# An adaLN block with a decaying scan and a mixture of experts: the bias of the first expert layer as four products in four row tiles

## The chip, the cores and the metric

The kernel runs on one core of one Trainium2 chip. The metric is the device time of one execution in microseconds; where several runs are shown, their median counts. The core's engines work side by side and wait for one another on semaphores: PE (matrix products; its weight loads are listed as PEld), DVE and ACT (element-wise work), POOL (here element-wise work and scatters), and SP, which issues most of the DMAs.

## The reference

x has 16 batches of 512 tokens with 128 features, 8192 tokens in all. The first half of the block (layer norm, modulation, a projection, a decaying scan over the tokens, a projection back) isn't touched. In the second half each token is normalised again, and a router picks two of eight experts for it. What matters is what an expert e computes for its tokens h, with D = 128 and F = 512:

```python
p = softmax(xt @ Wr + br); probs, idx = top_k(p, 2); probs = probs / probs.sum(-1)
h = einsum('td,edf->etf', xt, W1) + b1[:, None, :]
h = layernorm(relu(h), g1, be1)
y = einsum('etf,efd->etd', h, W2) + b2[:, None, :]
y = layernorm(relu(y), g2, be2)
out = einsum('te,etd->td', gate, y)
```

The first bias b1, one row of 512 numbers per expert, is what the change is about.

## The kernel before

**Stages.** A mixer stage runs over the 16 batches (`mixer_step`, from about 0 to 165 us): it computes the first half of the block, the router, and for each token and choice a row in DRAM (`expert_rows`), sorted by expert. Then an expert stage runs over 135 tiles of 128 rows (`expert_step`, s from 0 to 141, `EXPERT_TILES` = 135); each tile belongs to one expert, whose number is known only on the chip, so engines read it into registers (`load_expert`, `load_expert_numbers`). At the end the two results of each token are weighted and added to x.

**A tile on its way.** Each engine has its own list of work for step s, written by hand; a tile passes through several steps.
- SP loads the rows of tile i (`load_rows`, line 504) into one of 8 slots, and the shifts of its expert (`load_shifts`, line 515). `load_next(i)` first waits until the tile that had the slot, i - 8, has been turned (t3_done) and has its target numbers (target_ready). Tables of row and expert numbers are read for four tiles at once.
- PE turns the rows (`turn_rows`, line 1553, for tile s + 2). ACT copies them rounded (`high_part`, h3hi, line 765), DVE makes the rest (`low_part`, h3lo, line 1140), so that the product with W1, itself in a high and a low part, keeps its precision.
- PE computes h of tile s (`hidden`, lines 1555 to 1564): b1 first, then three products of 512 columns, all into one of two PSUM banks, 1 and 2. b1's product (line 1561) multiplies a matrix of ones with `b1_parts`, a tile of 128 rows that holds b1 of all experts: row 0 its high part, row 1 its low part, zeros in the other rows.
- ACT takes h out of its bank with a relu (`hidden`, line 769, for tile s - 1, r_ready); PE turns it in four transposes (`turn_hidden`, line 1569, for tile s - 2) into bank 3 or 0; ACT copies that to rT (line 773, tile s - 3); DVE takes statistics of r (line 1145) and their mean and variance (line 1391).
- PE computes the second layer of tile s - 4 (line 1672, four products that show as eight) into bank 4 or 5; DVE scales and shifts it (`values`, line 1362, tile s - 5), ACT applies the relu (line 870), DVE takes statistics (lines 1381 and 1386), ACT takes a square root for the norms of two tiles (line 882), DVE a reciprocal, and ACT and POOL end the second norm (lines 878 and 662). POOL scatters the tile to `expert_results` (line 674).
- From tile 53 on, `piece_tile` (lines 246 to 248) spreads 44 pieces of work over the steps, each of which sums two results for 128 tokens: ACT weights the first (`early_y0g`, line 845, at the end of its step), DVE adds the second (line 1453). SP loads the results for them (line 558).

**The order on each engine.** In step s PE does h of tile s, the turn of the rows of s + 2, the second layer of s - 4, the transposes of s - 2. ACT does h3hi of s + 1, the relu of h of s - 1, the relu of s - 5, the copy to rT of s - 3, the scaling of s - 8, the square root, then a piece. DVE does the values of s - 5, the reciprocal, the scaling, h3lo, and the statistics; it ends with the targets of tile s and a piece.

**The start.** ACT fills `b1_parts` with zeros (line 747, eight copies). `split_b1` (line 749) splits b1, and SP copies the two parts into rows 0 and 1 (lines 462 and 463). Tiles 0 and 1 (`EARLY_H` = 2) are begun in the mixer's last steps: `hidden(0)` and `hidden(1)` run in its steps B and B + 1.

## Time and profile before

| | us |
|---|---|
| median of three runs | 515.25 |
| the three runs | 515.25, 514.6, 516.82 |
| the profiled execution: span from its first to its last instruction | 512.1 |
| PE busy in the span | 486.5 (95%) |
| DVE busy | 440.3 (86%) |
| ACT busy | 420.4 (82%) |
| POOL busy | 364.3 (71%) |

For the profiled execution the page gives the span; the runs' times also hold what lies before the first instruction and after the last. Busy times of PE overlap with those of its weight loads, and the products are pipelined, so the distance from one start to the next tells what a product costs, not its length. In the rows below a line is the line of the kernel before.

### The profile page before, as it was taken

What the parts mean: (1) busy time and instruction counts of PE and PEld (TensorE: products, weight loads), DVE (VectorE), ACT (ScalarE), POOL (GpSimd) and SP (SyncE); (2) the same over time, 40 slices, a digit from 0 to 9 for tenths busy, and PEclk for the clock granted to TensorE, in tenths of its full rate; (3) what the DMA queues carried; (4) which work ended last, traced back from release to release, by engine and by line L of the source; (5) the groups of instructions that cost most, each with busy time, mean ns of one, the idle gap of its engine ahead of it and who ended that gap; (6) DMA issues with size and microseconds to landing.
All of it is one profiled execution on the core that took longest, in us unless ns stands there. A gap on an engine that the chain in (4) does not pass through costs nothing. (4 is left out here: it accounts for less than half of the span.)

```text
span 512.1 us, 14684 instructions
## 1 busy us (share of the span) xinstructions
PE 486.5 (95%) x3051; PEld 386.3 (75%) x3051; DVE 440.3 (86%) x2217; ACT 420.4 (82%) x1148; POOL 364.3 (71%) x483
## 2 busy tenths in 40 slices
PE   7989999999985899999999999999999999999994
PEld 6446656555544798998989799998999989999951
DVE  7779899998887698888888799988989999898894
ACT  6678887978764688888888798899989889999883
POOL 1004665666667778888888888888888888888871
PEclk9999999999997899999999999999999999999998
DMA  6980111145111789677515785677677677567555
GB/s 166 312 240 27 44 47 48 47 131 111 55 44 52 166 154 172 188 191 198 163 64 158 187 221 152 184 205 176 164 207 191 162 189 206 151 187 214 164 173 164
DMA packets 79786, 77.78 MB, mean 152 GB/s; under 512 B 11150, under 2 KB 72745, under 8 KB 79702
## 3 DMA queue, kind: packets, MB, share of 16 engines
q1 hardware_dynamic: 71286, 59.92, 47.2%
q0 software_dynamic: 8416, 16.93, 9.2%
q8 instruction: 29, 0.48, 0.3%
q14 instruction: 55, 0.45, 0.3%
HBM read 54.65 MB, written 22.59 MB: 151 GB/s over the span
## 5 line engine op out<-in xcount | busy, mean ns | idle before, releaser
L646 POOL DMA_INDIRECT expert_rows<-rows_ring,slot x128 | 123.3, 963 | 93.6 <-issue 76.3
L674 POOL DMA_INDIRECT expert_results<-y,target x119 | 123.0, 1034 | 30.7 <-issue 26.2
L1672 PE MATMUL bank<-W,h2T 128*128 x720 | 95.4, 275 | 0.8 <-ACT h2T L773 0.3
L1672 PEld LDWEIGHTS bank<-W,h2T 128*128 128x128 f32 x720 | 87.7, 192 | 9.1 <-issue 1.4
L870 ACT ACTIVATE v<-wmod 128x128 f32<-128x128 f32 x135 | 42.0, 311 | 39.1 <-DVE vg L1373 35.5
L1362 DVE SCALAR_TENSOR_TENSOR wmod<-bank,rse,shifts 128x128 f32<-128x128 f32 x119 | 41.6, 350 | 30.8 <-PE bank L1672 25.9
L1561 PE MATMUL bank<-b_parts,onesr 128*128 x135 | 64.9, 481 | 1.2 <-DVE h3lo L1140 1.2
L758 ACT ACTIVATE n<-X,nm,rs 128x128 f32<-128x128 f32 x128 | 54.1, 486 | 8.0 <-DVE nm L1307 8.0
L1145 DVE BATCH_NORM_STATS2 stf<-h1T 128x6 f32<-128x512 f32 x90 | 59.2, 658 | 0.0
L1569 PE MATMUL bank<-ident_wr,h1T 128*128 128x128 f32 x360 | 54.5, 274 | 0.0
L1562 PE MATMUL bank<-W1hi,h3hi 128*128 x135 | 53.8, 399 | 0.0
L1563 PE MATMUL bank<-W1lo,h3hi 128*128 x135 | 53.7, 398 | 0.0
L1564 PE MATMUL bank<-W1hi,h3lo 128*128 x135 | 53.6, 397 | 0.0
L769 ACT ACTIVATE h1T<-bank 128x512 f32<-128x512 f32 x90 | 53.0, 589 | 0.2 <-PE bank L1564 0.2
L773 ACT ACTIVATE h2T<-bank 128x512 f32<-128x512 f32 x90 | 52.3, 581 | 0.1
L1672 PE MATMUL bank<-W,third_rT 128*128 x360 | 47.6, 275 | 0.8 <-ACT third_rT L773 0.8
L1672 PEld LDWEIGHTS bank<-W,third_rT 128*128 128x128 f32 x360 | 43.7, 192 | 4.9 <-issue 1.0
L1569 PEld LDWEIGHTS bank<-ident_wr,h1T 128*128 128x128 f32 x360 | 42.9, 142 | 0.3 <-issue 0.2
L1373 DVE SCALAR_TENSOR_TENSOR vg<-v,mve,shifts 128x128 f32<-128x128 f32 x119 | 42.5, 357 | 0.0
L882 ACT ACTIVATE sde<-mve,eps 128x2 f32<-128x2 f32 (+1 forms) x138 | 40.6, 295 | 0.9 <-DVE mve L1386 0.7
L1140 DVE TENSOR_TENSOR h3lo<-bank,h3hi 128x128 fp32r<-128x128 f32 x135 | 37.9, 281 | 2.8 <-ACT h3hi L765 2.8
L1381 DVE BATCH_NORM_STATS2 sty<-v 128x6 f32<-128x128 f32 x135 | 38.0, 281 | 0.3 <-ACT v L870 0.2
(250 smaller groups left out, 1229.0 us busy)
## 6 DMA issues: line engine op xcount, KB each, us to landing
shifts<-expert_shifts SPq DMA_DIRECT2D x119, 192.0 KB
hrow<-expert_rows SPq DMA_DIRECT2D x135, 65.0 KB
xi<-expert_results SPq DMA_DIRECT2D x12, 512.0 KB, 5.3
out_x<-X SPq DMA_DIRECT2D x15, 256.0 KB
X<-in_L_attn_x SPq DMA_DIRECT2D x7, 512.0 KB, 7.4
W1lo<-in_L_ffn_W SPq DMA_DIRECT2D x4, 512.0 KB, 6.7
expert_rows<-rows_ring,slot POOLq DMA_INDIRECT x128
expert_results<-y,target POOLq DMA_INDIRECT x119
```

The costliest lines, as they stand in the source:

```text
L646: nc.gpsimd.indirect_dma_start(out=rows_d, out_offset=bass.IndirectOffsetOnAxis(ap=slot[q][:, n // TOPK, n % TOPK:n % TOPK + 1], axis=0), ...
L674: nc.gpsimd.indirect_dma_start(out=results_d, out_offset=bass.IndirectOffsetOnAxis(ap=target[i % TARGETS][:], axis=0), in_=y[k], in_offset ...
L758: ins = nc.scalar.activation(dst[:, j:j + 1, :], X[:, bass.ds(b * J + j, 1), :], ACT.Identity, bias=nm_[:, x_tiles + j:x_tiles + j + 1], s ...
L769: nc.scalar.activation(r[i % DEPTH], bank[1 + i % 2][:], ACT.Relu).then_inc(r_ready, 1)
L773: nc.scalar.activation(rT[i % DEPTH], bank[3 * (1 - i % 2)][:], ACT.Copy).then_inc(rT_ready, 1)
L1145: vec.bn_stats(stf[i % 2][:], r[i % DEPTH]).then_inc(stf_ready, 1)
L1561: mm(h, onesr[:], b1_parts[:, bass.ds(e, 1), :], start=True, stop=False)
L1562: mm(h, h3hi[i % DEPTH], W1hi[:, bass.ds(e, 1), :], start=False, stop=False)
L1563: mm(h, h3hi[i % DEPTH], W1lo[:, bass.ds(e, 1), :], start=False, stop=False)
L1564: mm(h, h3lo[i % DEPTH], W1hi[:, bass.ds(e, 1), :], start=False, stop=True).then_inc(h_done, 1)
L1569: ins = tr(bank[3 * (1 - i % 2)][:, ch * P:(ch + 1) * P], r[i % DEPTH][:, ch * P:(ch + 1) * P], ident[:])
L1672: ins = mm(acc, rT[(s - 4) % DEPTH][:, ch * P:(ch + 1) * P], W2[:, bass.ds(e4 * CF + ch, 1), :], start=(ch == 0), stop=(ch == CF - 1))
```

## The change

- b1's two parts go to DRAM (`b1_two_parts`) instead of to rows of a large tile; the zeros on ACT go.
- SP loads the two rows (high and low, 4 KB) of each tile's expert into `b1_ring`, at rows 0, 32, 64 and 96 for four successive tiles, with two turns; a group of four is loaded eight tiles ahead, by `load_b1`, called in `load_next` ahead of the load of the rows. It waits for h_done of the tile eight before.
- PE issues b1's products for four tiles together (`biases`) when i is a multiple of 4: each multiplies two rows of ones with two rows of b1, each in its own quarter of the rows, each into its own bank. There are four h banks (1, 2, 3, 0) instead of two. `biases(i)` waits for the loads and for r_ready, i, which says that h of tiles up to i - 1 has been taken out.
- Turned tiles have one bank, 4, instead of two, and the second layer has one, 5; `turn_hidden` waits for the last copy to rT, and the second layer for the last values.
- In a step s that is a multiple of 4 ACT takes out h of tile s - 1 before it makes h3hi of tile s + 1.
- Some semaphores are merged (sums_stored and spare_stored go into others).

```diff
--- before.py
+++ after.py
@@ -63,6 +63,7 @@
     sums_d = nc.dram_tensor("column_sums", (2, E, D), F32, kind="Internal").ap()
     shifts_d = nc.dram_tensor("expert_shifts", (E, 3 * D), F32, kind="Internal").ap()
     gates_d = nc.dram_tensor("gate_b_rows", (1, B * D), F32, kind="Internal").ap()
+    b1_d = nc.dram_tensor("b1_two_parts", (E, 2, F), F32, kind="Internal").ap()
 
     with ExitStack() as ctx:
         def sb(name, shape, dt=F32):
@@ -116,7 +117,9 @@
         w2_sums = means[0:2, 0:E, :]
         third_rT = sb("third_rT", [P, F], F32R)
         b1hi = third_rT[0:E, :]
-        b1_parts = sb("b1_parts", [P, E, F], F32R)
+        TOGETHER = 4
+        QUARTER = P // TOGETHER
+        b1_ring = sb("b1_ring", [P, 2, F], F32R)
         onesr = sb("onesr", [P, P], F32R)
         onesf = sb("onesf", [P, P])
         WIDE = P + E
@@ -281,6 +284,27 @@
 
             return max((m for m in range(i) if ring(m) == ring(i)), default=None)
 
+        def together(i):
+
+            return range(i, min(i + TOGETHER, EXPERT_TILES))
+
+        def b1_rows(i):
+
+            first = i % TOGETHER * QUARTER
+            return slice(first, first + 2), i // TOGETHER % 2
+
+        def b1_count(i):
+
+            return 16 * sum(len(together(n)) for n in range(i % (2 * TOGETHER), i + 1, 2 * TOGETHER))
+
+        hidden_banks = [bank[n] for n in (1, 2, 3, 0)]
+
+        def hidden_bank(i):
+
+            return hidden_banks[i % len(hidden_banks)]
+
+        turned_bank, value_bank = bank[4], bank[5]
+
         early01 = [t[:].rearrange("p c l -> p (c l)").rearrange("p (j k) -> p j k", j=J) for t in xi]
         early_gb = [t[:, :].rearrange("p (j d) -> p j d", j=J) for t in scan]
         idle_rows = rows_ring[:].rearrange("p k j r -> p (k j r)")
@@ -310,10 +334,10 @@
         shifts_loaded = [sem(f"shifts_loaded{n}") for n in range(SLOTS)]
         b2_loaded = sem("b2_loaded")
         w1hi_ready, w1lo_ready = sem("w1hi_ready"), sem("w1lo_ready")
-        spare_stored = sem("spare_stored")
         pool_consts = sem("pool_consts")
         dve_setup, act_setup, pe_setup = sem("dve_setup"), sem("act_setup"), sem("pe_setup")
         gb_stored, gb_loaded, b1_stored = sem("gb_stored"), sem("gb_loaded"), sem("b1_stored")
+        b1_loaded = [sem(f"b1_loaded{n}") for n in range(2)]
 
         (n1_ready, t1_done, h1T_ready, xi0_done, xi1_done, xi0_ready, xi1_ready, z_done,
          scan_ready, mix_ready, mix_done) = [sem(n) for n in (
...
@@ -451,31 +475,31 @@
             sp.dma_start(gates_d.rearrange("o (b d) -> (o b) d", b=B), gb_raw[:]).then_inc(gb_stored, 16)
 
             sp.wait_ge(sums_copied, 2)
-            sp.dma_start(sums_d, w2_sums).then_inc(sums_stored, 16)
+            sp.dma_start(sums_d, w2_sums).then_inc(shifts_stored, 16)
             sp.dma_start(shifts_d[:, 0:D].rearrange("(o e) d -> o e d", o=1), w2_sums[0:1, :, :]).then_inc(shifts_stored, 16)
-            sp.wait_ge(sums_stored, 16)
-            sp.wait_ge(shifts_stored, 16)
+            sp.wait_ge(shifts_stored, 32)
             sp.dma_start(means[:, 0:E, :], sums_d[1:2].broadcast_to([P, E, D])).then_inc(sums_loaded, 16)
 
             sp.wait_ge(dve_setup, SETUP_END)
-            sp.wait_ge(act_setup, 3)
-            sp.dma_start(b1_parts[0:1, :, :].bitcast(F32), b1hi.bitcast(F32)).then_inc(b1_stored, 16)
-            sp.dma_start(b1_parts[1:2, :, :].bitcast(F32), b1lo[:].bitcast(F32)).then_inc(b1_stored, 16)
+            sp.wait_ge(act_setup, 2)
+            sp.dma_start(b1_d[:, 0, :], b1hi.bitcast(F32)).then_inc(b1_stored, 16)
+            sp.dma_start(b1_d[:, 1, :], b1lo[:].bitcast(F32)).then_inc(b1_stored, 16)
 
             sp.wait_ge(dve_setup, SETUP_PADDING)
             for n in range(NSPARE):
-                sp.dma_start(rows_d[SPARE + n * P:SPARE + (n + 1) * P, :], padding[:]).then_inc(spare_stored, 16)
+                sp.dma_start(rows_d[SPARE + n * P:SPARE + (n + 1) * P, :], padding[:]).then_inc(padding_stored, 16)
 
             for n, src in ((0, g2_in), (1, be2_in)):
                 sp.dma_start(second_gains[n], src).then_inc(second_gains_loaded, 16)
             sp.wait_ge(second_gains_loaded, 32)
             for n in range(2):
                 sp.dma_start(shifts_d[:, (1 + n) * D:(2 + n) * D], second_gains[n]).then_inc(shifts_stored, 16)
-            sp.wait_ge(shifts_stored, 48)
+            sp.wait_ge(shifts_stored, 64)
             sp.wait_ge(w1lo_ready, E)
 
             sp.wait_ge(table_ready, 1)
             AT_ONCE = 4
+            assert TOGETHER == AT_ONCE
             row_of, expert_of = {}, {}
 
             def load_row_numbers(i):
@@ -505,11 +529,18 @@
 
             SHIFT_LAG = SLOTS - 2
 
+            def load_b1(i):
+                load_expert_numbers(i)
+                if i == 0:
+                    sp.wait_ge(b1_stored, 32)
+                if i >= 2 * TOGETHER:
+                    sp.wait_ge(h_done, i - 2 * TOGETHER + 1)
+                for n in together(i):
+                    part, turn = b1_rows(n)
+                    sp.dma_start(b1_ring[part, turn, :].bitcast(F32), b1_d[bass.ds(expert_of[n], 1), :, :].rearrange("o k f -> (o k) f")
+                                 ).then_inc(b1_loaded[turn], 16)
+
             def load_shifts(i):
-                if i % AT_ONCE == 0:
-                    load_expert_numbers(i)
-                if i == SLOTS:
-                    sp.wait_ge(b1_stored, 32)
                 if last_user(i) is not None:
                     sp.wait_ge(y_ready, last_user(i) + 1)
                 sp.dma_start(shift_rows[ring(i)], shifts_d[bass.ds(expert_of[i], 1), :].broadcast_to([P, 3 * D])).then_inc(shifts_loaded[shift_lane(i)], 16)
@@ -517,6 +548,7 @@
             def load_next(i):
                 if i % AT_ONCE == 0:
                     load_row_numbers(i)
+                    load_b1(i)
                 sp.wait_ge(t3_done, i + 1 - SLOTS)
                 sp.wait_ge(target_ready, i + 1 - SLOTS)
                 load_rows(i, i % SLOTS)
@@ -524,6 +556,8 @@
 
             for n in range(SLOTS):
                 load_rows(n, n)
+            for n in range(0, SLOTS, TOGETHER):
+                load_b1(n)
             for n in range(SLOTS - SHIFT_LAG):
                 load_shifts(n)
             count_of = {}
@@ -574,8 +608,7 @@
             LOADED_AT = {piece_tile(b, 0) + 1: b for b in range(EARLY)}
             for i in range(ROUND1, EXPERT_TILES):
                 if i == LAST_ROWS:
-                    sp.wait_ge(spare_stored, 16 * NSPARE)
-                    sp.wait_ge(padding_stored, 16 * E)
+                    sp.wait_ge(padding_stored, 16 * (NSPARE + E))
                     rows_of_batches(B)
                 load_next(i)
                 if i in GB_AT:
@@ -742,10 +775,7 @@
 
             act.wait_ge(c_loaded, 16)
             nc.scalar.activation(c_act[:], c_sb[:], ACT.Silu).then_inc(act_setup, 1)
-            act.wait_ge(dve_setup, SETUP_PADDING)
-            for e in range(E):
-                ins = nc.scalar.activation(b1_parts[:, e, :], padding[:, TAGS:TAGS + 1].broadcast_to([P, F]), ACT.Copy)
-            ins.then_inc(act_setup, 1)
+
             def split_b1():
                 act.wait_ge(gains_loaded, 80)
                 act.wait_ge(dve_setup, SETUP_PADDING)
@@ -766,11 +796,11 @@
 
             def hidden(i):
                 act.wait_ge(h_done, i + 1)
-                nc.scalar.activation(r[i % DEPTH], bank[1 + i % 2][:], ACT.Relu).then_inc(r_ready, 1)
+                nc.scalar.activation(r[i % DEPTH], hidden_bank(i)[:], ACT.Relu).then_inc(r_ready, 1)
 
             def hidden_turned(i):
                 act.wait_ge(tr_done, i + 1)
-                nc.scalar.activation(rT[i % DEPTH], bank[3 * (1 - i % 2)][:], ACT.Copy).then_inc(rT_ready, 1)
+                nc.scalar.activation(rT[i % DEPTH], turned_bank[:], ACT.Copy).then_inc(rT_ready, 1)
 
             def mixer_step(s, q, e, k):
                 if on(s, B):
@@ -855,11 +885,14 @@
 
             def expert_step(s, n):
                 q = n % 2
+                last_of_group = s % TOGETHER == 0
+                if last_of_group and on(s - 1, EXPERT_TILES) and s - 1 >= EARLY_H:
+                    hidden(s - 1)
                 if on(s + 1, EXPERT_TILES) and s + 1 >= EARLY_H:
                     high_part(s + 1, bank[7 - q][:, 0:P])
                 if s == 1:
                     half_gates()
-                if on(s - 1, EXPERT_TILES) and s - 1 >= EARLY_H:
+                if not last_of_group and on(s - 1, EXPERT_TILES) and s - 1 >= EARLY_H:
                     hidden(s - 1)
                 if on(s - 3, EXPERT_TILES) and s >= EXPERT_TILES:
                     hidden_turned(s - 3)
@@ -972,7 +1005,7 @@
                 vec.tensor_scalar(be1_g1m[:, :, 1], bank[7][:, 0:E * CF], 1.0 / F, None, ALU.mult)
                 mark(vec.tensor_copy(be1_g1m[:, :, 0], bank[7][:, E * CF:2 * E * CF]))
                 assert done[0] == SETUP_SUMS
-                dve.wait_ge(act_setup, 3)
+                dve.wait_ge(act_setup, 2)
                 mark(vec.tensor_tensor(b1lo[:], b1f[:], b1hi, ALU.subtract))
                 assert done[0] == SETUP_END
 
@@ -1359,7 +1392,7 @@
                 dve.wait_ge(y_done, s - 4)
                 dve.wait_ge(shifts_loaded[shift_lane(s - 5)], 16 * shift_uses(s - 5))
                 dve.wait_ge(rse_ready, s - 4)
-                vec.scalar_tensor_tensor(wide(v0[p]), wide(bank[4 + p][:, 0:D]), rse[q][:, 0:1],
+                vec.scalar_tensor_tensor(wide(v0[p]), wide(value_bank[:, 0:D]), rse[q][:, 0:1],
                                          wide(shift_rows[k5][:, 0:D]), ALU.mult, ALU.add).then_inc(v0_ready, 1)
 
             def reciprocals(s, p):
@@ -1552,21 +1585,30 @@
                 pe.wait_ge(hrow_loaded[row_slot], (i + SLOTS - row_slot) * (16 // SLOTS))
                 tr(to, hrow[row_slot][:, H], ident[:]).then_inc(t3_done, 1)
 
+            def biases(i):
+                pe.wait_ge(b1_loaded[i // TOGETHER % 2], b1_count(i))
+                pe.wait_ge(r_ready, i)
+                for n in together(i):
+                    part, turn = b1_rows(n)
+                    mm(hidden_bank(n)[:], onesr[part, :], b1_ring[part, turn, :], start=True, stop=False)
+
             def hidden(i):
-                e, q = expert_of[i], i % 2
-                h = bank[1 + q][:].rearrange("p (o f) -> p o f", o=1)
+                e = expert_of[i]
+                h = hidden_bank(i)[:].rearrange("p (o f) -> p o f", o=1)
+                if i == 0:
+                    pe.wait_ge(h3lo_ready, EARLY_H)
+                if i % TOGETHER == 0:
+                    biases(i)
                 pe.wait_ge(h3lo_ready, i + 1)
-                if i >= 2:
-                    pe.wait_ge(r_ready, i - 1)
-                mm(h, onesr[:], b1_parts[:, bass.ds(e, 1), :], start=True, stop=False)
                 mm(h, h3hi[i % DEPTH], W1hi[:, bass.ds(e, 1), :], start=False, stop=False)
                 mm(h, h3hi[i % DEPTH], W1lo[:, bass.ds(e, 1), :], start=False, stop=False)
                 mm(h, h3lo[i % DEPTH], W1hi[:, bass.ds(e, 1), :], start=False, stop=True).then_inc(h_done, 1)
 
             def turn_hidden(i):
                 pe.wait_ge(r_ready, i + 1)
+                pe.wait_ge(rT_ready, i)
                 for ch in range(CF):
-                    ins = tr(bank[3 * (1 - i % 2)][:, ch * P:(ch + 1) * P], r[i % DEPTH][:, ch * P:(ch + 1) * P], ident[:])
+                    ins = tr(turned_bank[:, ch * P:(ch + 1) * P], r[i % DEPTH][:, ch * P:(ch + 1) * P], ident[:])
                 ins.then_inc(tr_done, 1)
 
             def mixer_step(s, q, e, k):
@@ -1661,10 +1703,10 @@
                     load_expert(s + 1)
                 if on(s - 4, EXPERT_TILES):
                     e4 = expert_of[s - 4]
-                    acc = bank[4 + q][:, 0:D].rearrange("p (o d) -> p o d", o=1)
+                    acc = value_bank[:, 0:D].rearrange("p (o d) -> p o d", o=1)
                     pe.wait_ge(rT_ready, s - 3)
-                    if on(s - 6, EXPERT_TILES):
-                        pe.wait_ge(v0_ready, s - 5)
+                    if on(s - 5, EXPERT_TILES):
+                        pe.wait_ge(v0_ready, s - 4)
                     if s == TABLE2_STEPS:
                         pe.wait_ge(spread_ready, 2)
                         mm(bank[5][:, TABLE:TABLE + 2 * P], onesf[:], spread[:].rearrange("p t i -> p (t i)"), start=True, stop=True).then_inc(spread_done, 1)
```

## Rows read from the trace of the kernel before

**Rows 1.** Section 1 of the page: busy us of each engine, share of the span, instructions.
```profile
PE 486.5 (95%) x3051; PEld 386.3 (75%) x3051; DVE 440.3 (86%) x2217; ACT 420.4 (82%) x1148; POOL 364.3 (71%) x483
```

**Rows 2.** Windows, expert stage: busy us (x instructions) PE, PEld, DVE, ACT, POOL; clock, DMA.
```profile
172.00:488.00 316.00, 315.15 (x2256) 284.85 (x2254) 279.00 (x1245) 277.36 (x829) 265.06 (x373) 1.00 0.68 177
```

**Rows 3.** Timeline of PE, one step: start us, us, engine, line, op [idle before <-releaser].
```profile
299.97 0.60 PE L1569 MATMUL bank<-ident_wr,h1T 128*128 128x128 f32 x4
...
302.34 0.60 PE L1569 MATMUL bank<-ident_wr,h1T 128*128 128x128 f32 x4
302.69 0.47 PE L1561 MATMUL bank<-b_parts,onesr 128*128 x1
303.00 0.39 PE L1562 MATMUL bank<-W1hi,h3hi 128*128 x1
...
303.70 0.27 PE L1553 MATMUL bank<-ident_wr,hrow 128*128 128x128 f32 x1
303.81 1.06 PE L1672 MATMUL bank<-W,h2T 128*128 x8
304.70 0.60 PE L1569 MATMUL bank<-ident_wr,decay 128*128 128x128 f32 x4
```

**Rows 4.** Timeline of PE and its loads: transposes of 32 rows; full loads.
```profile
17.31 0.60 PE L1539 MATMUL bank<-ident_wr,n 128*128 128x128 f32 x4
...
17.84 0.13 PEld L1522 LDWEIGHTS bank<-ident_wr,rows_ring 32*128 32x128 f32 x1 [0.17 <-issue]
...
17.90 0.14 PEld L1523 LDWEIGHTS bank<-ident_wr,rows_ring 32*128 32x128 f32 x1
...
302.67 0.19 PEld L1561 LDWEIGHTS bank<-b_parts,onesr 128*128 128x128 f32 x1
...
302.78 0.19 PEld L1562 LDWEIGHTS bank<-W1hi,h3hi 128*128 128x128 f32 x1
```

**Rows 5.** Timeline of DVE and ACT in the steps of rows 3.
```profile
300.17 0.35 DVE L1362 SCALAR_TENSOR_TENSOR wmod<-bank,rse,shifts 128x128 f32<-128x128 f32 x1 [0.35 <-PE bank L1672]
...
301.82 0.16 DVE L1386 BATCH_NORM_AGGREGATE mve<-sty 128x2 f32<-128x6 f32 x1
...
302.22 0.26 ACT L765 ACTIVATE h3hi<-bank 128x128 fp32r<-128x128 f32 x1
...
302.38 0.59 ACT L769 ACTIVATE h1T<-bank 128x512 f32<-128x512 f32 x1
...
302.54 0.35 DVE L1362 SCALAR_TENSOR_TENSOR wmod<-bank,rse,shifts 128x128 f32<-128x128 f32 x1
...
303.52 0.58 ACT L773 ACTIVATE h2T<-bank 128x512 f32<-128x512 f32 x1
...
304.59 0.39 ACT L845 ACTIVATE n<-xi,gate 128x128 f32<-128x128 f32 x1
...
304.88 0.26 ACT L765 ACTIVATE h3hi<-bank 128x128 fp32r<-128x128 f32 x1
```

**Rows 6.** Timeline of ACT and PE at the last tiles.
```profile
487.43 0.57 ACT L773 ACTIVATE h2T<-bank 128x512 f32<-128x512 f32 x1
...
488.15 1.22 PE L1672 MATMUL bank<-W,h2T 128*128 x8 [0.28 <-ACT h2T L773]
```

**Rows 7.** SP's waits in total (us, times, longest); timelines: an SP issue, a late row load.
```profile
SPq L515 <- POOL y L662: 96.4, 85, 9.9
...
305.65 0.33 SPq L504 DMA_DIRECT2D hrow<-expert_rows  x1
...
291.29 0.33 PE L1553 MATMUL bank<-ident_wr,hrow 128*128 128x128 f32 x1 [0.25 <-DMA hrow<-expert_rows]
```

**Rows 8.** Timeline of ACT and DVE at the start.
```profile
3.43 4.26 ACT L747 ACTIVATE b_parts<-padding 128x512 fp32r<-128x512 f32 x8 [0.81 <-DVE padding L940]
...
7.15 0.16 DVE L1307 SCALAR_TENSOR_TENSOR nm<-mv,rs 128x4 f32<-128x4 f32 x1
```

**Rows 9.** Timeline of PE's weight loads, end of the mixer stage.
```profile
159.57 0.42 PEld L1539 LDWEIGHTS bank<-ident_wr,n 128*128 128x128 f32 x4 [0.55 <-ACT n L758]
```

More of the change, by code:

```diff
@@ L334, in adaln_ssm_moe_kernel @@
         rows_stored = [sem(f"row_group_stored{m}") for m in range(ROW_LANES)]
-        sums_done, sums_copied, sums_stored, sums_loaded, w2_ready = (
-            sem("sums_done"), sem("sums_copied"), sem("sums_stored"), sem("sums_loaded"), sem("w2_ready"))
+        sums_done, sums_copied, sums_loaded, w2_ready = (
+            sem("sums_done"), sem("sums_copied"), sem("sums_loaded"), sem("w2_ready"))
         count_done, counts_ready, table_step, spread_ready, spread_done, table_ready, padding_stored = (
```

## The prediction

> **What bounds the kernel now.** I read the busy shares first: PE is at 95%, DVE, ACT and POOL lie under it [rows 1]. A share is a mean over stages, so I asked for the stretch in which the expert tiles run: from 172 to 488 us PE is busy 315.15 of 316.00 us at a granted clock of 1.00, while DVE and ACT are busy 279 and 277 [rows 2]. In that stretch PE is the bound and the others wait for it. The timeline of PE then gives the step of one tile [rows 3]: transposes of r at 302.34, b1's product at 302.69, three W1 products from 303.00, the turn of the next rows at 303.70, the second layer at 303.81, the next tile's transposes at 304.70. That is 2.36 us from transposes to transposes, with no idle time noted on any row; 133 tiles at 2.36 make 314 us, which is the stretch.
>
> **The change, part by part. b1's product leaves the step.** The start noted for the first product of a tile comes early, since its weights are still being loaded; so I take the pitch of the three behind it: 303.70 - 303.00 = 0.70, 0.233 each [rows 3]. Tiles 2 to 134 lose one each: 133 x 0.233 = **-31.0 us**. Nothing on PE covers it, so all of it lies on the path; the step becomes 2.13.
>
> **Four b1 products together, 33 times** (before tiles 4, 8, ..., 132). No product in four row tiles stands in the trace, so I bound it. From below: one load and one product's pitch, all four side by side, no cost for going over to row tiles and back: 0.06 + 0.23 = 0.29. From above: one load at the full pitch, four products one after the other, and a drain: 0.11 + 4 x 0.23 + 0.09 = 1.12. The nearest rows are the two transposes of 32 rows, which also use only part of the array's rows [rows 4]. They show two things. The load for the second starts 0.06 after the load for the first (17.84, 17.90), while full loads stand 0.11 apart (302.67, 302.78). And the first 32-row load starts only at 17.84, though four transposes at 0.11 each from 17.31 have fed their last column by 17.75: 0.09 for draining before the change of rows, and the trace notes no engine that it waited for. I take loads one after the other at 0.06, products side by side, and one drain on the way back: 4 x 0.06 + 0.23 + 0.09 = **0.56 per group**. The drain on the way in is hidden by the wait that comes next; without that cover 0.09 more.
>
> A rule of the Trainium skill, page "TensorE: Matmul & The Clock Gate", section "LDWEIGHTS (loading the stationary operand)", says that a load's time goes with its columns and that 32 rows take as long as 128. By that rule the four loads cost 0.44 instead of 0.24 and the sum is that of the rival of slow loads, below. The 0.06 in the trace speaks against it, but it is one pair of loads.
>
> **A new wait on PE.** The four products write all four h banks, so they wait (r_ready, i) until ACT has taken out the h of the tile just before. PE's transposes at 299.97 stand two steps before the b1 product at 302.69 [rows 3]; without b1's product in between, PE is there after 2.72 - 0.23 = 2.49 us. ACT's chain in the same time [rows 5]: DVE's values start at 300.17, released by PE's second layer; DVE's last statistics of the step start at 301.82; ACT's step ends with a square root of them, and its next step starts at 302.22, 2.25 after the transposes. There h3hi comes first now and h at 302.38; the change puts h first in each fourth step, so h is out at 2.25 + 0.59 = 2.84. From ACT's end to PE's next load the tail of the trace shows 488.15 - (487.43 + 0.57) = 0.15 [rows 6], with a register operation in between, which the four products do not have; with 0.10, PE starts at 2.94. **The wait is 2.94 - 2.49 = 0.45 per group** (0.40 to 0.50). The chain hangs on PE's own second layer two steps back, for which DVE was waiting (0.35 idle), so a faster PE does not shorten it. Behind the wait stands all of PE's work and, through it, DVE's and ACT's; SP and POOL run ahead. Where ACT also does y0g in the step before (304.59, with the next start at 304.88), the wait grows by 0.29; by lines 246 to 248 this is so for seven groups (after tiles 83, 87, ..., 107): +2.0 us. In the fourth step h3hi goes up to 0.59 later; its reader on PE is a step away.
>
> **The other waits.** One bank for turned tiles: PE's transposes also wait for the last rT. ACT's copy ends at 303.52 + 0.58 = 304.10, the transposes start at 304.70 [rows 3, 5]; ACT's copy follows DVE's values, and these PE's step, so that of 0.60 at least 0.37 stays. One bank for values: DVE is done at 302.54 + 0.35, PE wants the bank at 303.81: 0.92 of cover. If a cover fell short by 0.1 in every step it would cost 13 us; I see no reason for it. At the end, where PE's steps have no hidden layer, the single bank bites: the last transposes must wait for ACT's copy until 488.00, and the second layer of 488.15 goes back by their length [rows 6]: +0.3 us (0 to 0.5).
>
> **SP and the DMAs.** 135 loads of 4 KB come in, four per group, at SP's place just before the load of tile i's rows; reading the experts' numbers moves there too, and h_done of tile i-8 is awaited there. Behind it stand the rows of tile i and the shifts of tile i-6. SP waits 96.4 us for POOL's y alone, and 135 issues of 0.33 are 45 us [rows 7]; target_ready of tile i-8, awaited there already, comes later than h_done. I cost it at nothing. If the cover fails, rows come late as at 291.29, 0.25 idle [rows 7]: at the eleven early loads of results (line 558) up to 11 x 0.25 = 2.8 us.
>
> **Start and change of stage.** ACT's eight fills of b1_parts (4.26 us from 3.43, so until 7.69) go; ACT's next work waits for nm, ready at 7.15 + 0.16 [rows 8]: -0.2 us (0 to -0.4). The first group is issued in the mixer's last steps and waits for the second h3lo; soon after, PE idles 0.55 at 159.57 for ACT [rows 9], which covers that and the products. Without that cover, up to 0.5.
>
> **The sum.** -31.0 + 33 x (0.56 + 0.45) + 2.0 + 0.3 - 0.2 = +4.4 us. It is made against the profiled execution, a span of 512.1; the timed runs stand at 514.6 to 516.82, about 3 us above it, and I add the difference to their median: 515.25 + 4.4 = **519.7 us**. With the bounds of the wait and of the late ends this case holds 516.5 to 524. A measurement here tells about 0.5%, 2.6 us, from no change. So the group's price decides: at 0.43 nothing changes, under 0.35 it is faster by 0.5%, over 0.50 slower by it.
>
> **Rivals.**
> *Loads side by side too.* Different rows of the array could load at once: 0.11 + 0.23 + 0.09 = 0.43, 33 x -0.13 = -4.3, 515.4 us, no change. For it: the 0.06 was for two loads into the same rows, so it need not hold between different rows. Against it: no full loads overlap in the trace. The same page of the Trainium skill, section "Measured speedup vs the span model", gives four row tiles 3.07 times the speed of one after the other; by it, as an estimate, 4 x 0.23 / 3.07 + 0.09 = 0.39 and 514.1 us. No row here shows four.
> *Faster.* Everything side by side and no drain: the lower bound, 0.29, 33 x -0.27 = -8.9, 510.8 us. The wait remains even so, which is why there is no more to be had. For it: the 0.09 may belong to something else than the change to 32 rows. Against it: it is the place where PE goes to fewer rows at full clock, and it shows the gap.
> *Slow loads.* Four at 0.11: 0.76, 33 x 0.20 = +6.6, 526.3 us. For it: every full load that follows another stands 0.11 behind it. Against it: the pair at 0.06.
> *The change doesn't do what it says.* The products run one after the other: 1.12, 33 x 0.56 = +18.5, 538.2 us. For it: the products of 512 columns in these rows are 0.23 or more apart. Against it: those use the whole array.
>
> **Chances.** Forecast 0.40, loads side by side 0.22, faster 0.12, slow loads 0.12, one after the other 0.14. The wait's uncertainty (0.05 x 33 = 1.7 us) spreads the first two over the bounds of 0.5%: faster by over 0.5% 0.12 + 0.06 = 0.18, within 0.24, slower by over 0.5% 0.58. The range goes from 510.0, just past the faster case, to 530.0, past slow loads; it leaves out products one after the other and a little at each end, under 0.2.
>
> **What would show it.** Right: no b1 product in three of four steps, and those steps at 2.13; in the fourth, PE idle 0.35 to 0.5 ahead of its load, released by ACT's relu (longer where y0g stands before it), four products whose starts are some 0.06 apart, and the first W1 load 0.56 after the first b1 load; DVE's wait for PE shorter in three steps. Wrong: no idle time there (the chain through DVE was not tight), starts 0.23 apart (no row tiles), steps without b1 longer than 2.13 (DVE, ACT or a bank took over), or rows that come late.

## The result and the profile after

The changed kernel takes 520.69 us (median of four runs, 519.55 to 522.04) against 515.42 (514.6 to 516.82) for the kernel before beside it: a ratio of 1.0103, 95% interval 1.0074 to 1.0131. It is slower by about 1%, 5.3 us; the forecast was 4.4 us slower. The profiled execution ran 521.47 us with a span of 519.6. That is 7.5 us above the span of 512.1 before: the two profiled executions lie further apart than the medians, and what is read from the profiles below adds up to these 7.5.

In the new lines, b1's products are L1593, the W1 products L1603 to L1605, the turn of the rows L1586, the second layer L1714, the transposes of r L1611; on ACT h3hi is L795, the relu of h L799, y0g L875.

The busy times of the page, and the same window as in [rows 1, 2]:

```profile
PE 483.3 (93%) x3051; PEld 371.7 (72%) x3051; DVE 442.1 (85%) x2217; ACT 413.8 (80%) x1140; POOL 360.9 (69%) x483
172.00:488.00 316.00, 302.40 (x2200) 261.72 (x2199) 273.70 (x1216) 268.89 (x813) 255.39 (x364) 1.00 0.67 176
```

In the expert stage PE, idle for 0.85 us before, now stands idle for 316.00 - 302.40 = 13.6 us, and fewer instructions fit into the same window, on every engine. The timeline of PE, a step without b1 and a step with a group, answers [rows 3]:

```profile
346.04 0.60 PE L1611 MATMUL bank<-ident_wr,h1T 128*128 128x128 f32 x4
346.39 0.48 PE L1603 MATMUL bank<-W1hi,h3hi 128*128 x1
...
347.18 0.27 PE L1586 MATMUL bank<-ident_wr,hrow 128*128 128x128 f32 x1
347.29 1.05 PE L1714 MATMUL bank<-W,third_rT 128*128 x8
348.18 0.60 PE L1611 MATMUL bank<-ident_wr,h1T 128*128 128x128 f32 x4
349.04 0.51 PE L1593 MATMUL bank<-b_ring,onesr 2*128 2x512 f32 x4 [0.27 <-ACT h1T L799]
349.48 0.49 PE L1603 MATMUL bank<-W1hi,h3hi 128*128 x1
...
351.29 0.60 PE L1611 MATMUL bank<-ident_wr,decay 128*128 128x128 f32 x4
```

The step without b1 takes 348.18 - 346.04 = 2.14, as worked out. The step with a group takes 351.29 - 348.18 = 3.11, 0.97 more. All four products together last 0.51 from the first start to the last end, hardly longer than one alone (0.47 in [rows 3]): they run side by side. PE's weight loads at the same place:

```profile
349.01 0.22 PEld L1593 LDWEIGHTS bank<-b_ring,onesr 2*128 2x128 f32 x4 [0.47 <-issue]
349.48 0.19 PEld L1603 LDWEIGHTS bank<-W1hi,h3hi 128*128 128x128 f32 x1 [0.25 <-issue]
```

The four loads also run side by side: 0.22 for all four, against 0.19 for one full load. From the first of them to the next full load it is 0.47, of which 0.25 is idle time of the loads without a releaser. The products run in this time, 0.23 for one by its pitch, so the 0.25 is not the price of the way back alone. From the first b1 product to W1 it is 0.44, 0.21 more than one product's pitch; how much of that is loads and how much the way back isn't told apart. ACT's timeline shows what PE waits for, at this group and at one with y0g before it:

```profile
348.12 0.29 ACT L915 ACTIVATE sde<-mve,eps 128x2 f32<-128x2 f32 x1
348.31 0.59 ACT L799 ACTIVATE h1T<-bank 128x512 f32<-128x512 f32 x1
348.78 0.28 ACT L795 ACTIVATE h3hi<-bank 128x128 fp32r<-128x128 f32 x1
...
387.80 0.39 ACT L875 ACTIVATE n<-xi,gate 128x128 f32<-128x128 f32 x1
388.09 0.57 ACT L799 ACTIVATE h1T<-bank 128x512 f32<-128x512 f32 x1
```

The square root, then h, first in the step, out at 348.90; PE's load follows at 349.01. Where y0g stands between them, PE's row is

```profile
388.81 0.50 PE L1593 MATMUL bank<-b_ring,onesr 2*128 2x512 f32 x4 [0.56 <-ACT h1T L799]
```

an idle time of 0.56 instead of 0.27. Two rows of a tile come late, as in [rows 7] but by more:

```profile
293.25 0.33 PE L1586 MATMUL bank<-ident_wr,hrow 128*128 128x128 f32 x1 [0.59 <-DMA hrow<-expert_rows]
...
299.09 0.33 PE L1586 MATMUL bank<-ident_wr,hrow 128*128 128x128 f32 x1 [0.80 <-DMA hrow<-expert_rows]
```

**Where the time went.** I add up the distances between starts on PE from tile 4's first W1 product to tile 134's, 130 steps:

| | us |
|---|---|
| before | 310.1 |
| b1's product gone from 130 steps, 0.227 each | -29.5 |
| 32 groups: last transpose to first b1 product, and from there to W1, 33.8 in all, less the 0.03 that a step without a group has there | +32.9 |
| before and after the turn of the rows (late rows) | +2.0 |
| small delays elsewhere (what is left over) | +1.5 |
| after | 317.0 |

The median distance from one tile's first W1 product to the next tile's tells the kernels apart (g: the step into a tile whose b1 products come first in a group; each profile has some longer steps besides):

| kernel | step | step g | g in every |
|---|---|---|---|
| before | 2.37 | | |
| after | 2.15 | 3.15 | 4th |
| groups of four, the last h taken out early | 2.16 | 2.76 | 4th |
| groups of three, no wait | 2.16 | 2.75 | 3rd |
| groups of two, no wait | 2.16 | 2.75 | 2nd |

### The profile page after: what moved, and what is told of

The parts are those of the page before. It is cut to its first block and busy times, and to the rows that moved or that the text cites. A ratio compares the mean times of both kernels' runs of the same rounds, so it can differ in the third digit from the quotient of the medians.

```text
span 519.6 us, 14981 instructions
## 1 busy us (share of the span) xinstructions
PE 483.3 (93%) x3051; PEld 371.7 (72%) x3051; DVE 442.1 (85%) x2217; ACT 413.8 (80%) x1140; POOL 360.9 (69%) x483
## 5 line engine op out<-in xcount | busy, mean ns | idle before, releaser
L707 POOL DMA_INDIRECT expert_results<-y,target x119 | 120.2, 1010 | 30.0 <-issue 24.0
L1714 PE MATMUL bank<-W,h2T 128*128 x720 | 95.5, 276 | 1.1 <-issue 0.6
L1714 PEld LDWEIGHTS bank<-W,h2T 128*128 128x128 f32 x720 | 87.5, 191 | 10.0 <-issue 2.3
L1603 PE MATMUL bank<-W1hi,h3hi 128*128 x135 | 66.6, 494 | 0.7 <-DVE h3lo L1173 0.7
L1611 PE MATMUL bank<-ident_wr,h1T 128*128 128x128 f32 x360 | 54.4, 274 | 0.0
L1605 PE MATMUL bank<-W1hi,h3lo 128*128 x135 | 54.1, 401 | 0.0
L799 ACT ACTIVATE h1T<-bank 128x512 f32<-128x512 f32 x90 | 52.8, 587 | 1.1 <-PE bank L1605 1.1
L1714 PE MATMUL bank<-W,third_rT 128*128 x360 | 47.8, 276 | 1.0 <-DVE wmod L1395 0.8
L1714 PEld LDWEIGHTS bank<-W,third_rT 128*128 128x128 f32 x360 | 43.7, 191 | 5.7 <-issue 1.8
L1611 PEld LDWEIGHTS bank<-ident_wr,h1T 128*128 128x128 f32 x360 | 42.1, 142 | 0.9 <-issue 0.4
L1586 PE MATMUL bank<-ident_wr,hrow 128*128 128x128 f32 x135 | 36.9, 276 | 1.4 <-DMA hrow<-expert_rows 1.4
```

Source lines behind the costliest of these rows:

```text
L707: nc.gpsimd.indirect_dma_start(out=results_d, out_offset=bass.IndirectOffsetOnAxis(ap=target[i % TARGETS][:], axis=0), in_=y[k], in_offset ...
L799: nc.scalar.activation(r[i % DEPTH], hidden_bank(i)[:], ACT.Relu).then_inc(r_ready, 1)
L1603: mm(h, h3hi[i % DEPTH], W1hi[:, bass.ds(e, 1), :], start=False, stop=False)
L1605: mm(h, h3lo[i % DEPTH], W1hi[:, bass.ds(e, 1), :], start=False, stop=True).then_inc(h_done, 1)
L1611: ins = tr(turned_bank[:, ch * P:(ch + 1) * P], r[i % DEPTH][:, ch * P:(ch + 1) * P], ident[:])
L1714: ins = mm(acc, rT[(s - 4) % DEPTH][:, ch * P:(ch + 1) * P], W2[:, bass.ds(e4 * CF + ch, 1), :], start=(ch == 0), stop=(ch == CF - 1))
```

## The experiments

**1. Four products in one row tile.** Are the row tiles worth what they seem?

```diff
 def b1_rows(i):
-    first = i % TOGETHER * QUARTER
-    return slice(first, first + 2), i // TOGETHER % 2
+    return slice(0, 2), i % (2 * TOGETHER)
```

> The changed kernel with one edit: b1's two rows of all four tiles lie at row 0, so the four products of a group use the same row tile. Theory 1 (row tiles make the products run side by side): in the changed kernel the group takes 0.44 us from the first b1 load to the first W1 load, starts 0.003 apart; here starts 0.21 to 0.23 apart, the group 0.11 + 4 x 0.23 + 0.09 = 1.12, so 33 x 0.68 = +22 us over the changed kernel's 520.7: about 543 us. Rival (the group's price is the going over to few rows and back, whichever rows they are): starts and price as in the changed kernel, 520.7 us.

548.66 us (546.97 to 550.1), ratio 1.0651 (1.0612 to 1.0691). Timeline of PE (lines are one lower here):

```profile
301.53 1.16 PE L1592 MATMUL bank<-b_ring,onesr 2*128 2x512 f32 x4 [0.31 <-ACT h1T L798]
302.62 0.50 PE L1602 MATMUL bank<-W1hi,h3hi 128*128 x1
```

In one row tile the four last 1.16 together and W1 follows 302.62 - 301.53 = 1.09 after the first; in four row tiles it is 0.44. 33 times 0.65 is 21.5 of the 28.0 us; in the expert stage the granted clock is also 0.98 in this profile, not 1.00, which is about 6 us of 316. Theory 1 holds, with 28 us instead of 22: the row tiles do what they say.

**2. The relu of h in its old place.**

```diff
-    last_of_group = s % TOGETHER == 0
+    last_of_group = False
```

> The changed kernel without its last part: ACT makes h3hi first and takes out h after it in every step. Theory 1 (PE waits at each group for h of the tile before, at the end of the chain second layer, DVE, ACT): h comes out one h3hi later, 0.16 us by the starts of the two, so PE's wait grows from 0.48 to 0.64 per group: 33 x 0.16 = +5.3 us, about 526 us. Rival (PE's wait ends on something else, the b1 loads or PE's own queue): no change, 520.7 us within 1.5.

528.41 us (526.89 to 530.98), ratio 1.0275 (1.023 to 1.0321). The waits of this kernel, and those of the changed kernel (us, times, longest):

```profile
PE bank L1593 <- ACT h1T L799: 11.1, 21, 0.9
PE bank L1593 <- ACT decay L799: 5.8, 11, 0.9
```

```profile
PE bank L1593 <- ACT h1T L799: 7.7, 21, 0.7
PE bank L1593 <- ACT decay L799: 3.7, 11, 0.6
```

The new order on ACT is worth 7.7 us, 5.5 of them (16.9 - 11.4) in this one wait. PE does hang on ACT's relu, and the length of ACT's work ahead of it sets the wait.

**3. The wait without the products, and neither.** Both leave b1 out of h.

```diff
 for n in together(i):
     part, turn = b1_rows(n)
-    mm(hidden_bank(n)[:], onesr[part, :], b1_ring[part, turn, :], ...)
+    pass
 ...
-mm(h, h3hi[i % DEPTH], W1hi[...], start=False, stop=False)
+mm(h, h3hi[i % DEPTH], W1hi[...], start=True, stop=False)
```

> The changed kernel without the four b1 products (b1 is left out of the result); the waits ahead of them stay. Theory 1: the group's 0.44 goes, the wait of 0.48 stays: 520.7 - 33 x 0.44 = about 506 us. Rival (the products hide in the wait or the wait grows in their place): 515 us or more.

514.02 us (512.63 to 515.64), ratio 0.9976 (0.996 to 0.9992): 6.7 us less than the changed kernel, half of the 14 expected, and between the two cases. Timeline of PE, two late rows and a group:

```profile
271.20 0.33 PE L1586 MATMUL bank<-ident_wr,hrow 128*128 128x128 f32 x1 [1.85 <-DMA hrow<-expert_rows]
...
275.70 0.47 PE L1586 MATMUL bank<-ident_wr,hrow 128*128 128x128 f32 x1 [0.53 <-DMA hrow<-expert_rows]
...
310.24 0.60 PE L1611 MATMUL bank<-ident_wr,h1T 128*128 128x128 f32 x4
311.14 0.49 PE L1603 MATMUL bank<-W1hi,h3hi 128*128 x1 [0.29 <-issue]
```

At the group, 0.90 from the transposes to W1 instead of 0.35 elsewhere (346.39 - 346.04): the wait alone is 0.55. Over the 25 groups from tile 8 on that have no y0g ahead of them the median is 0.54; in the changed kernel, with the products, the same 25 have 0.48. So the wait is there without the products, and they don't lengthen it. The steps with a group fall from 3.15 to 2.75 in the median, as the price of the products says; but with faster steps two rows come later, and those two steps take 5.13 and 4.07, 4.9 us more than 2.15 each.

The second kernel loosens the wait as well, to `pe.wait_ge(r_ready, i - 3)`, which one bank needs.

> The changed kernel without the four b1 products (b1 is left out of the result) and with the wait loosened to what a bank needs: h of four tiles before instead of one. Theory 1: the wait's 0.48 per group goes too, and the longer waits at pieces on ACT with it, 33 x 0.48 + 4 = 20 us less than with the wait: about 486 us, 133 steps of 2.14. Rival (without the wait DVE or ACT bounds the step, so that the wait costs little by itself): within 6 us of the kernel that keeps the wait, 500 us or more.

505.62 us (504.5 to 507.7), ratio 0.9818 (0.9777 to 0.9859): the wait is worth 8.4 us here, not the 20 of theory 1, and a little more than the rival's 6. Timeline of PE, then windows (PE, PEld, DVE, ACT, POOL; clock, DMA):

```profile
263.78 0.39 PE L1606 MATMUL bank<-W1hi,h3lo 128*128 x1
270.90 0.48 PE L1586 MATMUL bank<-ident_wr,hrow 128*128 128x128 f32 x1 [6.74 <-DMA hrow<-expert_rows]
271.47 2.07 PE L1715 MATMUL bank<-W,third_rT 128*128 x8
...
200.00:266.00 66.00, 64.11 (x473) 57.78 (x472) 59.29 (x262) 59.10 (x177) 55.48 (x72) 1.00 0.66 169
266.00:276.00 10.00, 5.01 (x18) 3.92 (x18) 3.94 (x18) 3.48 (x11) 8.60 (x12) 0.52 0.39 111
```

One row comes 6.74 late, and after this idle time PE's granted clock is at its lower level, 1.2 GHz: the second layer takes 2.07 instead of 1.05. So even a kernel with no b1 at all gains only 9.4 us over the one before, where 133 products of 0.227 are 30. PE's steps are not all that stands behind the time. SP's and POOL's timelines show what made this row late:

```profile
250.56 0.33 SPq L528 DMA_DIRECT2D hrow<-expert_rows  x1
267.40 0.33 SPq L546 DMA_DIRECT2D shifts<-expert_shifts  x1
267.96 0.33 SPq L528 DMA_DIRECT2D hrow<-expert_rows  x1
...
252.96 0.47 POOL L695 TENSOR_TENSOR xi<-wmod,mixT_both 128x128 f32<-128x128 f32 x1
257.55 0.46 POOL L695 TENSOR_TENSOR xi<-win,scan 128x128 f32<-128x128 f32 x1
```

SP's load of shifts waits for POOL's y of an earlier tile, and the loads of rows stand behind it. POOL works through its own list, two tiles in 257.55 - 252.96 = 4.59 us, so 2.3 a tile, with no idle time over 0.3 between its instructions there: nearly the 2.37 of PE's step in the kernel before, and more than the 2.15 here. In every kernel here but that of experiment 1, whose PE is the slowest, POOL's store of tile 42's results begins at 291.0 to 292.4 us, and at tile 56 none is ahead of the kernel before: the first W1 product of that tile starts at 298.3 there and at 299.7 in this one. The 9.4 us all come behind it. That POOL's list holds PE back up to there is read from the traces; no run took work from POOL.

**4. h of a group's last tile taken out early.** ACT does that relu in the step before, behind the copy to rT and ahead of the scaling and the square root. Products and group stay.

```diff
+    if (s + 1) % TOGETHER == 0 and s + 1 < EXPERT_TILES:
+        hidden(s)
```

> The changed kernel with one edit on ACT: h of the last tile of a group is taken out one step earlier in ACT's list, after the copy to rT and ahead of the scaling and the square root, so ahead of ACT's wait for DVE. Theory 1 (the wait of 0.48 per group hangs on the chain second layer, DVE's statistics, ACT's square root, h): h is out before PE arrives, PE's wait falls to 0.1 or less, 33 x 0.4 + 4 = -14 to -19 us: 502 to 507 us; DVE's reciprocal comes up to 0.3 later in one step of four, which DVE's wait for PE covers. Rival (the square root now comes 0.48 late and DVE hands it on to PE's second layer): the wait moves to the second layer and half or more of it stays, 512 to 521 us.

515.66 us (514.85 to 516.78, 12 runs), ratio 1.0006 (0.9995 to 1.0018): 5.0 us less than the changed kernel, in the rival's range and not in that of theory 1. The wait is gone, at every group. Timeline of PE and two windows of this kernel, then one of the changed kernel (PE, PEld, DVE, ACT, POOL; clock, DMA):

```profile
450.08 0.63 PE L1611 MATMUL bank<-ident_wr,h1T 128*128 128x128 f32 x4
450.64 0.51 PE L1593 MATMUL bank<-b_ring,onesr 2*128 2x512 f32 x4
451.08 0.50 PE L1603 MATMUL bank<-W1hi,h3hi 128*128 x1
...
172.00:180.00 8.00, 8.00 (x30) 6.34 (x30) 3.90 (x20) 3.28 (x9) 6.15 (x7) 0.50 0.72 169
360.00:480.00 120.00, 119.77 (x867) 102.87 (x866) 114.60 (x486) 107.39 (x333) 97.97 (x155) 1.00 0.70 195
```

```profile
172.00:180.00 8.00, 7.77 (x59) 6.77 (x58) 5.60 (x29) 5.63 (x16) 6.02 (x7) 1.00 0.81 175
```

With no releaser named, PE still starts the first b1 product 0.20 after the last transpose (median of 32 groups), where W1 starts 0.03 after it in other steps. That is 0.17 for going over to row tiles, which the wait had covered before. A group then costs 0.17 + 0.44 = 0.61 beyond the plain step, and four tiles save 0.91: 33 x 0.61 - 133 x 0.227 = -10 us should remain against the time of before. They don't. Three things in this profile stand against it. PE runs at the lower clock from 172 to 180 us, right behind the change of stage with its short stretches of work between waits: 30 products there against 59 in the changed kernel (last row). From tile 66 on the step before a group takes 2.35 to 2.41 instead of 2.14 in 10 of 17 cases, and some steps with a group are longer by 0.1: DVE is busy 114.60 of 120 us there, and the second layer and the transposes, which have one bank each, start a little late. And one row comes late (1.4 us in its step). By the steps' lengths these are some 3.4, 3.7 and 1.4 us; that the single banks are what passes DVE's and ACT's lateness on was not tried by itself. Nor does the clock decide it. The mean granted clock is 0.972 to 0.975 in five of the twelve runs and 0.978 to 0.981 in seven, and both take 515.8 us in the mean. The last kernel of experiment 7 has the same early relu and a clock of 0.99 from 172 to 180 us; its steps from tile 46 to 54, where rows come late, are 6 us longer in all, and it takes the same time. What fits both is POOL's pace up to tile 56: there this kernel starts at 299.0, against 298.3 before, and from there to tile 134 it takes 184.7 us, against 184.8.

**5. Three together on four banks.** A group of three leaves a bank over, so that its products need only the tile before the last (`pe.wait_ge(r_ready, i - 1)`); ACT keeps the order of before. b1's rows are loaded by threes too, two tiles later in SP's list.

```diff
-    TOGETHER = 4
+    TOGETHER = 3
...
-    pe.wait_ge(r_ready, i)
+    pe.wait_ge(r_ready, i - 1)
```

> The changed kernel with groups of three tiles on the four h banks: the products of a group then need h of the tile two before, not of the tile just before. ACT takes out h in its old place. Theory 1 (a group's wait is what eats the gain): no wait, 0.43 for each of 44 groups, so against the kernel before -31 + 44 x 0.43 = -12 us: about 503 us. Rival (each going over to row tiles costs PE more than the trace shows, or DVE and ACT bound the step): 512 us or more.

514.48 us (513.46 to 516.33, 12 runs), ratio 0.999 (0.9977 to 1.0003): the wait is gone here too, and no more is gained. Timeline of PE and a window:

```profile
335.61 0.60 PE L1612 MATMUL bank<-ident_wr,h1T 128*128 128x128 f32 x4
336.14 0.50 PE L1594 MATMUL bank<-b_ring,onesr 2*128 2x512 f32 x3
336.57 0.50 PE L1604 MATMUL bank<-W1hi,h3hi 128*128 x1
...
172.00:180.00 8.00, 8.00 (x43) 6.67 (x43) 4.59 (x23) 4.41 (x14) 6.17 (x7) 0.73 0.87 164
```

Three products cost the same 0.43 as four, so 44 groups at 0.60 give 26.4 back of the 30.2 saved. Theory 1 left the way in out of its price, and the 3.8 us that are left should show; 0.8 do, with an interval that holds no change. The clock stands at 0.73 behind the change of stage, but here too the time doesn't follow the mean clock of the run (four at 0.975 and 0.976 take 513.5 to 514.2, seven at 0.978 and 0.979 take 514.2 to 515.7, one at 0.972 takes 516.3).

**6. Two together.** If a group has a price of its own, groups of two must lose. Like experiment 5, with 67 groups, each in two row tiles (`pe.wait_ge(r_ready, i - 2)`, `for n in range(i, min(i + 2, EXPERT_TILES))`); b1's rows are loaded by fours, two tiles later than in the changed kernel.

> b1's products in groups of two, 67 of them, on four banks, with no wait for the tile just before, and ACT in the order of before. Theory (a group costs PE some 0.61 us beyond a step without it, whatever it holds: 0.17 for draining on the way in and 0.43 for products and the way back): 22 or 23 groups more than in groups of three, 14 us more than those 514.5, so 526 to 530 us; transposes to first b1 product 0.20 and first b1 product to first W1 product about 0.42. Rival (the price goes with the products in the group): groups of two cost half, 512 to 517 us.

526.65 us (526.05 to 526.9), ratio 1.0219 (1.0198 to 1.024). Timelines of PE and of its loads:

```profile
301.03 0.60 PE L1613 MATMUL bank<-ident_wr,decay 128*128 128x128 f32 x4
301.56 0.50 PE L1595 MATMUL bank<-b_ring,onesr 2*128 2x512 f32 x2
301.99 0.50 PE L1605 MATMUL bank<-W1hi,h3hi 128*128 x1
...
303.79 0.60 PE L1613 MATMUL bank<-ident_wr,h1T 128*128 128x128 f32 x4
...
305.94 0.27 PE L1613 MATMUL bank<-ident_wr,h1T 128*128 128x128 f32 x1
...
301.56 0.18 PEld L1595 LDWEIGHTS bank<-b_ring,onesr 2*128 2x128 f32 x2 [0.17 <-issue]
301.99 0.19 PEld L1605 LDWEIGHTS bank<-W1hi,h3hi 128*128 128x128 f32 x1 [0.25 <-issue]
```

The same 0.43 and the same 0.17 and 0.25 of idle loads, for two products. A step with a group is 2.76 long, one without 2.15: 0.61, 67 times, is 40.9, less 30.2 saved: 10.7 us slower, and 11.2 were measured. The price hangs on the group, not on what is in it; the rival (half the price for half the products) is out.

**7. Three smaller suspects.** The piece of y0g behind h and not ahead of it, in the steps with a group:

> The changed kernel with one edit on ACT: where a piece of the results' sum stands at the end of the step before a group, it is done after h is taken out instead. Theory 1 (such a piece lengthens PE's wait by 0.29 to 0.35 at the seven groups after tiles 83 to 107, where the wait reads 0.8 to 0.98 instead of 0.48): -2 to -3 us, 517.7 to 518.7. Rival (the longer waits there come from something else, such as DVE's sums): 520.7 within 1.

519.74 us (517.31 to 522.47), ratio 1.0082 (1.0053 to 1.011), against 1.0103 (1.0074 to 1.0131) for the changed kernel. By its time this is the rival's case, though the intervals overlap. The traces settle the wait itself: at the seven groups the way from the last transpose to the first b1 product falls from 0.82 to 1.00 in the changed kernel to 0.48 to 0.71 here, 1.8 us in all. So y0g does lengthen the wait there, by 0.25 in the mean; in the time it doesn't show.

b1's loads issued on SP behind the tile's rows and shifts, and not ahead of them:

> The changed kernel with one edit on SP: the four b1 loads of a group are issued behind the row and shift loads of tile i instead of ahead of them. Theory 1 (SP's four more issues stand ahead of the rows after a big load of results and make two row loads later, PE's wait for rows grows from 0.5 before to 1.9 in the changed kernel): about 1 us less, 519 to 520. Rival (the rows come late from the big loads of results alone): no change, and PE's wait for rows stays at 1.4 or more.

521.22 us (519.66 to 523.62), ratio 1.0126 (1.01 to 1.0153): no gain, though no wait of PE names the load of rows in this profile (one turn of rows has 0.58 of idle time ahead of it without a releaser). These late loads together with the early relu of experiment 4, as the version that might beat both kernels:

> The version with h of a group's last tile taken out early, and b1's rows loaded after the tile's rows and shifts. Theory (late rows are one of the delays that ate the gain of the early relu): no wait of PE for hrow, 513 to 515 us, just below the time of before. Rival (what ate it are small waits for ACT and DVE and the drain on the way in, not SP): 515 to 516.5, as without it.

515.47 us (514.07 to 516.69, 12 runs), ratio 0.9994 (0.9979 to 1.0009): the time of the rival. Rows still come late, by up to 0.89 of idle time (0.89, 0.52, 0.67). The order of the loads on SP does not decide it. The waits of SP in the kernel of experiment 3 without wait and products point to POOL, whose y frees the shifts (us, times, longest; the 16.4 is the wait shown there):

```profile
SPq L546 <- POOL y L695: 43.1, 29, 16.4
```

No run took that wait away.

## Why the prediction was right, and where its steps were off

**The forecast's sum held by its total, not by its parts.** Slower by over 0.5% was the likeliest case and it came; 519.7 against 520.69. That it is so near is in part luck: the sum starts from the profiled execution before, and to the profiled execution after it the difference is 7.5 us, 3.1 more than forecast, while the medians lie 5.3 apart. By the profiles the group came out 4.1 us cheaper than forecast, the wait with y0g some 2.5 dearer, and the rest is what the sum had at nothing.

**b1's product out of the step, -31.0:** 133 x 0.227 = -30.2 by the steps. Right. No bank and no engine took over in the changed kernel: its steps without a group are 2.15 in the median.

**The group, 0.56: too high.** "I take loads one after the other at 0.06" failed. Loads and products run side by side, 0.22 and 0.51 for all four, and the group is 0.44, the figure of the first rival (0.43). The loads of [rows 4] at 0.06 went into the same rows, as the text had warned. What it held against the rival, that no full loads overlap, is not what [rows 4] show: the full load of 302.67 lasts until 302.86, and the next starts at 302.78. Side by side is shown by experiment 1, the fixed price by experiments 5 and 6.

**The wait, 0.45: right in kind and place, a little short.** It is 0.48 in the median of the 25 groups without y0g ahead of them; with the seven others the median of all 32 is 0.54. Experiment 3 has it without the products, so it is not their price, experiment 2 shows that it ends with ACT's relu, and in experiment 4 it goes when the relu goes ahead. Group and wait together are 0.97, forecast 1.01: the two errors nearly cancel. The first rival had the group's price right; what it lacked is the longer wait and the terms below that no sum had.

**"The drain on the way in is hidden by the wait; without that cover 0.09 more".** Hidden, yes; its size is 0.17 (experiments 4 to 6), and 0.17 is also the idle time that the row of [rows 4] notes, where the text worked out 0.09. The Trainium skill, page "TensorEngine Tiling (Array Packing)", section "Key Properties", says that a change of the tiling mode drains the engine; the trace agrees: 0.17 of idle loads on the way in, and 0.25 ahead of the first full load behind a group, both without a releaser.

**y0g's 0.29 at seven groups, +2.0:** seven groups wait longer than the median of the others, by 0.32 to 0.50, 2.7 in all. Right in kind and place, a little short.

**SP and the DMAs, nothing, up to 2.8 if the cover fails:** the cover failed in part; around the turn of the rows 2.0 us were added. **Tail, +0.3:** the time from the last hidden layer to the end grew by 0.2. **Start, -0.2:** tile 2's W1 starts at 168.74 instead of 168.25, 0.5 later, which is the bound for a group without cover.

**Not foreseen:** the small delays of 1.5 us. And what no sum here would have found: had the wait been avoided, the gain of 10 us would still not have come (experiment 4).

**The other rivals.** Faster, with no drain: excluded, the drain is there at every group. Slow loads: excluded by 0.22 for four. Products one after the other: excluded by the 0.51 for all four, and experiment 1, which is that case, takes 548.66 (forecast 538.2, without the fall of the clock, which is about 6 us).

## What to carry to other kernels

Count changes of tiling mode on PE, not products: here going over to row tiles and back costs 0.61 us, as much as 2.7 of the products that it replaces, whether two, three or four run together; so two lose, and by the steps three or four gain a little if nothing else is paid; no measured time here shows that gain. Products that open several banks at once wait for the last bank's reader; a bank more than the group, or the reader's work moved ahead, takes that wait away, and both are to be tried before the group itself is judged. And where the other engines are 84 to 88% busy in the stage [rows 2], a saving on the bound is worth its size only up to the next one: of the 10 us net that the steps promised without the wait, the measured times show nothing. Ask for each engine how long one tile takes it in its own list, stretch by stretch: POOL's 2.3 us up to tile 56 were hidden behind PE's 2.37 in the kernel before.

## What the runs showed of the hardware

- Loads of two rows into four different quarters of the array take 0.22 us for all four, two of them 0.18 (experiment 6), and one full load 0.19; four into the same rows take 0.75 (the load row of experiment 1):

```profile
301.50 0.75 PEld L1592 LDWEIGHTS bank<-b_ring,onesr 2*128 2x128 f32 x4 [0.52 <-issue]
```

- Four products of 512 columns in four row tiles: W1 0.44 behind the first, against 1.09 in one row tile, 2.5 times faster. The Trainium skill, page "TensorE: Matmul & The Clock Gate", section "Measured speedup vs the span model", has 3.07 times; no row here shows the products without the way back to full rows, which is in both of these figures.
- Going over to row tiles costs 0.17 us (0.20 from the last transpose to the first b1 product, where it is 0.03 to W1), and from that product to W1 it is 0.43 or 0.44: both the same for two, three and four products. No run tells the change of row tiles apart from the change to few rows.
- PE's granted clock fell to its lower level during an idle time of 6.74 us (1.00 until 266, 0.52 from 266 to 276 us), and from 172 to 180 us, behind the change of stage, it was 0.50 in one profile (experiment 4) and 1.00 in that of the changed kernel, whose work differs by the place of one relu. Why it differs there is open.
